# Activations of the gated and plain expert stages go to SBUF instead of back into their PSUM bank

## The reference, cut to what matters

```python
x = x + _L0_attn_ref(_layernorm(x), ...);  x = x + _L0_ffn_ref(_layernorm(x), ...)
x = x + _L1_attn_ref(_layernorm(x), ...);  x = x + _L1_ffn_ref(_layernorm(x), ...)
x = x + _L2_attn_ref(_layernorm(x), ...);  x = x + _L2_ffn_ref(_layernorm(x), ...)
x = x + _L3_attn_ref(_layernorm(x), ...);  x = x + _L3_ffn_ref(_layernorm(x), ...)
```

```python
# layer 0: 64 experts of width 64, two share a chunk of 128 rows; one shared expert without a routing weight
expert_act = silu(x @ gate[e]) * (x @ up[e])
routed = sum_e((expert_act * router_mask[..., e]) @ down[e])      # + shared expert
# layer 1: 8 experts of width 128
out = sum_e(cw[:, e] * (square(relu(x @ w1[e])) @ w2[e]))
# layer 2: 4 experts of width 512 (16 chunks of 128)
out = sum_i(w_i * (relu(x @ W1[e_i] + b1[e_i]) @ W2[e_i] + b2[e_i]))
# layer 3: 8 experts of width 128
out = sum_e(weights[..., e] * ((silu(x @ Wg[e]) * (x @ Wu[e])) @ Wd[e]))
```

## Time and profile before

| | us |
|---|---|
| median of 3 runs | 2436.68 |
| the profiled execution's own time | 2446.33 |
| its span | 2444.6 |
| PE busy | 1734.2 |
| DVE busy | 1528.8 |
| ACT busy | 1033.7 |
| POOL busy | 827.6 |

### The profile page before, as it was taken

The page is one execution under the profiler, slowest core; times in us unless marked ns, Lnnn a source line. Parts: engine busy times, 40 slices in busy tenths (PEclk is TensorE's granted clock), DMA queues, the critical chain, the costliest instruction groups (busy, mean ns, idle before and its releaser), DMA issues. The chain is left out here.

```text
span 2444.6 us, 31503 instructions
## 1 busy us (share of the span) xinstructions
PE 1734.2 (71%) x9106; PEld 1310.7 (54%) x9106; DVE 1528.8 (63%) x3384; ACT 1033.7 (42%) x1728; POOL 827.6 (34%) x717
## 2 busy tenths in 40 slices
PE   2903455666999999999577757767779994443599
PEld 2903355434777777777355535545546663222387
DVE  6787422355766666666546757767765566988566
ACT  0308400224544555554345635543447772222454
POOL 2020000002555555555300005530038783222255
PEclk9955565777999999999757758878879997665699
DMA  1001488106755555545100006430011111000355
GB/s 37 13 9 62 145 279 288 63 11 140 152 111 110 113 113 110 115 108 109 42 18 1 1 6 122 104 80 1 1 27 43 34 34 26 0 1 1 69 121 120
DMA packets 144435, 179.55 MB, mean 73 GB/s; under 512 B 37527, under 2 KB 89051, under 8 KB 144379
## 3 DMA queue, kind: packets, MB, share of 16 engines
q1 hardware_dynamic: 142568, 178.47, 30.5%
q10 hardware_dynamic: 1810, 0.42, 0.1%
HBM read 174.53 MB, written 4.33 MB: 73 GB/s over the span
## 5 line engine op out<-in xcount | busy, mean ns | idle before, releaser
L794 POOL TENSOR_TENSOR ffn_alo<-ffn_a,ffn_ahi 128x512 fp32r<-128x512 f32 x520 | 669.6, 1290 | 509.3 <-ACT ffn_ahi L755 505.6
L821 DVE TENSOR_TENSOR ffn_a<-ffn_G,ffn_mask 128x512 f32<-128x512 f32 x384 | 264.8, 690 | 241.6 <-ACT ffn_G L763 218.6
L763 ACT ACTIVATE ffn_G<-ffn_G 128x512 f32<-128x512 f32 x384 | 223.5, 582 | 359.0 <-PE ffn_G L104 356.9
L755 ACT ACTIVATE ffn_ahi<-ffn_a 128x512 fp32r<-128x512 f32 x520 | 324.7, 624 | 32.9 <-DVE ffn_a L825 29.0
L102 PE MATMUL ypsum<-ffn_ahi,ffn_hi 128*128 128x512 f32 x520 | 228.1, 439 | 48.7 <-POOL ffn_alo L794 34.9
L102 PE MATMUL ffn_G<-xn_hi,ffn_hi 128*128 (+1 forms) x520 | 220.8, 425 | 31.3 <-DVE ffn_lo L801 27.5
L825 DVE TENSOR_TENSOR ffn_a<-ffn_U,ffn_a 128x512 f32<-128x512 f32 x320 | 221.4, 692 | 29.7 <-DVE ffn_a L821 0.5
L194 POOL TENSOR_TENSOR ln_var<-ln_moments,eps 128x4 f32<-128x4 f32 x56 | 11.1, 199 | 671.2 <-DVE ln_moments L174 671.2
L103 PE MATMUL ffn_G<-xn_lo,ffn_hi 128*128 (+1 forms) x520 | 214.4, 412 | 0.0
L104 PE MATMUL ffn_G<-xn_hi,ffn_lo 128*128 (+1 forms) x520 | 213.8, 411 | 0.0
L103 PE MATMUL ypsum<-ffn_alo,ffn_hi 128*128 128x512 f32 x520 | 210.6, 405 | 0.0
(11 more groups left out here) (509 smaller groups left out, 3788.0 us busy)
## 6 DMA issues: line engine op xcount, KB each, us to landing
ffn_mask<-mask_rows_top SPq DMA_DIRECT2D x128, 512.0 KB, 6.8
rec_T<-scratch_kernels SPq DMA_DIRECT2D x32, 1536.0 KB, 7.7
ffn_mask<-mask_rows_top SPq DMA_DIRECT2D x16, 1024.0 KB, 8.2
ffn_mask<-mask_rows_zone SPq DMA_DIRECT2D x16, 1024.0 KB, 8.3
ffn_mask<-mask_rows_steps SPq DMA_DIRECT2D x16, 512.0 KB, 4.7
x<-in_L_attn_x SPq DMA_DIRECT2D x8, 256.0 KB, 4.8
ffn_raw<-in_L_ffn_expert_gate_k SPq DMA_DIRECT2D x16, 128.0 KB, 3.3
ffn_raw<-in_L_ffn_expert_up_k SPq DMA_DIRECT2D x16, 128.0 KB, 3.4
```

Of the source, the lines that this page charges most:

```text
L755: act.activation(ahi[i][:, :], a[i][:, :], ACT.Copy).then_inc(k.ahi_done, 1)
L763: act.activation(gate if masked(c) else a[c % RING_A][:, :], gate, how, **kw).then_inc(k.r_done, 1)
L794: eng.tensor_tensor(alo[i][:, :], a[i][:, :], ahi[i][:, :].bitcast(F32), ALU.subtract).then_inc(k.alo_done, 1)
L821: dve.tensor_tensor(out, gate[:, :], mask(c), ALU.mult).then_inc(k.t_done, 1)
```

## The change

In ffn0, ffn2 and ffn3 the activation is written to the chunk's buffer `a` in SBUF, and the first multiplication of DVE reads `a` and the mask, both in SBUF, and writes `a` in place. ffn1 stays as it was (`in_bank`). Two waits move with it: the wait for `alo_done` of chunk c - RING_A goes from DVE to ACT, ahead of the activation, and PE may write into a G bank as soon as the activation of the chunk RING_G before is done (`r_done`), no longer after DVE's multiplication. The wait of the up product for `a_done` stays.

```diff
+        in_bank = s.kind == "relu2"
         scaled = k.t_done if s.kind != "relu" else k.a_done
...
                     if exists(g, c, RING_G):
-                        if gated:
-                            pe.wait_ge(k.t_done, mid0 + g * C + c - RING_G + 1)
+                        if in_bank:
+                            pe.wait_ge(k.a_done, at(g, c) - RING_G + 1)
                         else:
-                            pe.wait_ge(k.a_done, at(g, c) - RING_G + 1)
+                            pe.wait_ge(k.r_done, at(g, c) - RING_G + 1)
...
                 def activate(g, c):
                     gate = banks(c)[0][:, :]
-                    if not masked(c) and exists(g, c, RING_A):
+                    if not in_bank and exists(g, c, RING_A):
                         act.wait_ge(k.alo_done, at(g, c) - RING_A + 1)
                     act.wait_ge(k.g_done, at(g, c) + 1)
                     kw = {"bias": bias1[:, c:c + 1]} if bias1 is not None else {}
-                    act.activation(gate if masked(c) else a[c % RING_A][:, :], gate, how, **kw).then_inc(k.r_done, 1)
+                    act.activation(gate if in_bank else a[c % RING_A][:, :], gate, how, **kw).then_inc(k.r_done, 1)
...
-                    if exists(g, c, RING_A):
+                    if in_bank and exists(g, c, RING_A):
                         dve.wait_ge(k.alo_done, at(g, c) - RING_A + 1)
+                    active = gate[:, :] if in_bank else out
                     if s.kind == "relu":
-                        dve.tensor_tensor(out, gate[:, :], mask(c), ALU.mult).then_inc(k.a_done, 1)
+                        dve.tensor_tensor(out, active, mask(c), ALU.mult).then_inc(k.a_done, 1)
                         return
-                    dve.tensor_tensor(out, gate[:, :], mask(c), ALU.mult).then_inc(k.t_done, 1)
+                    dve.tensor_tensor(out, active, mask(c), ALU.mult).then_inc(k.t_done, 1)
```

## The result

The changed kernel takes 2462.5 us in the median of 20 runs, the kernel before 2434.7 in as many beside it: a ratio of 1.010, 95% interval 1.0081 to 1.0119, so 20 to 29 us slower, 24 in the middle; the two medians themselves lie 27.8 us apart. The forecast was slower by 31 us, 2468 us, with a range of 2440 to 2502.

The account below looks back on a forecast made before the run. PE was taken to bound ffn0, ffn2 and ffn3, with DVE's two SBUF inputs contending with POOL deciding the change. ffn2 +25, ffn0 +7, ffn3 -0.7 sum to +31 us on 2436.7: 2468 us, range 2440 to 2502.

Parts of the forecast that it names:

- ffn3's -0.7: Start of ffn3: PE can do the third chunk's gate product before the late mask, -0.7 us, bounds -3.8 and 0.
- A pair costs 1.66 us: One DVE multiplication with two SBUF inputs plus one POOL subtraction, both engines always having work: 0.54 + 1.12 = 1.66 us.
- The sum of ffn2, +25: ffn2: +2.0 per group x 8 = +16, plus +1.3 at L181 for 7 groups = +9; bounds +6 and +75.
- One sign of being right: ffn2: PE was to wait for `alo` by some 20 us more than before.
- ffn0, +7: ffn0: multiplication falls into POOL's gap, leaving three terms of +2, +3 and +2 us; bounds 0 and +17.
- The part for the chunks behind the statistics, +3: ffn0, behind DVE's statistics, L181 and L216: later multiplication delays POOL 0.12 us x 3 places x 8 groups = +3.
- the +2 for it: ffn0: activation into SBUF takes 598 ns against 582; 8 ns a chunk x 264 = +2 us.
- the +2 at the inverse root: ffn0, where POOL is late already and PE waits 2.28 us: 0.25 us added a group, +2.
- Absorbed: Rival, 0.19: ffn2's multiplications slip into POOL's pauses as in ffn0; +2 to +8 us, 2441.
- Full blocking: Rival, 0.10: the second instruction waits, then takes its whole duration; 1.98 us a pair, ffn2 group 34.1 us, 2528 us.
- Clock: Rival, 0.06: ffn2's new waits drop PE's clock to 1.2 GHz once a group, +13 us on top, 2481.
- Faster: Rival, 0.05: gate bank given back 0.7 us earlier lets PE run ahead in ffn0, with ffn3 -15 us, 2422.

## Why the prediction was right, point by point

**The early bank release gives nothing.** Right. With ffn2 as before, the change in ffn0 and ffn3 has a ratio of 0.9987 with 1 inside the interval. ffn3's -0.7 did not show in the stages (0.0): PE's one wait of 3.8 us moved to the up product at its full length.

```profile
PE ffn_U L102 <- DVE ffn_a L827: 3.8, 1, 3.8
```

**A pair costs 1.66 us where both engines always have work.** Right: 15.12 / 9 = 1.68. The rows of an attention part with other operations on the same sizes carried over to this one, in both directions: a blocked multiplication ends 0.54 behind POOL's end, a blocked subtraction 1.14 behind DVE's.

**The sum of ffn2, +25.** Right in mechanism and, at +24.1, in size, but the nearness of the total is partly luck: a loop group was set 0.6 us too high, 4 us over seven groups, and the first group 3 us too low. A group was to take 29.0 us and 1.3 more in those with a normalisation, 30.3; it takes 29.7. The pause at the turn was set at 1.2 and is 1.46, the late chunk behind L181 at 1.3 and is a pause of 1.29. What was too high is POOL's busy time, 27.8 against 26.75: not all 16 multiplications are blocked, the one beside L196 (1872.16) takes 0.69, and three subtractions in a row in front of the late one need 1.26 each, as before. L194 on the other side is held too, 0.65 us where it took 0.20 before; that was not in the sum. The first group takes 5.0 us more from the attention's last copy to its own (60.5 against 55.5) where the sum gave it +2.0; which of its splits and multiplications make that up was not taken apart.

One sign of being right did not come as stated. PE was to wait for `alo` by some 20 us more in ffn2. By the profile it waits 8.3 us for `alo` (7.2 before) and 9.8 for `ahi` (0.8 before), the latter once a group behind the late multiplication, up to 1.3 us; the rest is spread in waits of some 0.2 us in front of the down products.

**ffn0, +7.** This term was mis-sized, and two of its three parts failed. The part for the chunks behind the statistics, +3, is the one that came. Four subtractions a group take 1.38 us and not 1.29 (754.10, where the prediction had worked out 0.12 more for just such a chunk), and the chunk behind each is 0.08 to 0.10 us longer. That is about 0.35 a group, all of what the undisturbed groups grew by (74.5 to 74.8 us). The activation's 16 ns were right in duration (598 against 582), but the other chunks of a group together did not grow, so the +2 for it does not show. Nor does the +2 at the inverse root: PE's wait there is 2.3 us as before, and L196 does not hold the multiplication inside it (0.69 to 0.70 us in all seven loop groups).

In the profile ffn0 even came out at -1.8. What hides the growth is the clock: the stall at the root was followed by a fall of the granted clock, some 1.5 us each, in four of the seven groups before and in two after. Whether the change has a part in that isn't settled. The other kernel with the change in ffn0, that with ffn2 as before, has two falls as well; the two with ffn0's activation in PSUM (the change in ffn2 alone, the wait alone moved) have four and three; each is one profile. The sign "within 1.5 us of 77" was set from a wrong base, too: 538 / 7 counts a window that runs on behind the last group, and the groups before took 75.2 on average.

**The rivals.** Absorbed: no, the mean multiplication of ffn2 is 1258 ns. Full blocking at 1.98 a pair: no, 1.68. Clock: a middle group of ffn2 kept 1.00 with PE's waits of up to 1.3 us in it. Faster: no. The forecast of 31 us lies 7 above the 24 of the ratio and of the stage table, and that is mostly the ffn0 term; it lies 3 above the 27.8 between the medians, so the runs don't fix the miss to the microsecond.

## What to carry to other kernels

Before moving an operand of VectorE from PSUM to SBUF, look at what GpSimd does at that time. If both inputs are in SBUF, the instruction and GpSimd's SBUF reads exclude each other, and there are two questions. Does the pair still fit the period of a chunk together with GpSimd's other work and pauses? In ffn2 it did not: 1.68 us a pair in a chunk of 1.69 left nothing for the inverse root and the turn of the group. And where does the instruction fall against GpSimd's? In ffn0, with 2.2 us a chunk, nearly all multiplications fell into POOL's gap; pushed onto the subtraction by a fill, they cost 5 to 6 us a group, though the pair is shorter than the chunk. In ffn3, with the same fill, a group kept its 17.2 us, so even this loss depends on what slack the stage has. Look for such a pair elsewhere in the same trace: it gives the price in both directions. And look at what stands behind a waiting instruction in GpSimd's list: one entry of a table was worth 18 us, with the same instructions.

## What the runs showed of the hardware that had not been expected

- Who goes first is not decided by the start of the rows. Behind a fill on DVE, a multiplication that started 0.62 us inside POOL's subtraction ran unhindered in 0.62 us and the subtraction took 2.38; behind L181, one that started 0.05 us inside it waited to its end. The cause is open.
- POOL's power function L196 on 128x4 did not hold a VectorE instruction with two SBUF inputs in its 1.01 us (0.69 to 0.70 us each time, in the 14 loop groups of ffn0 and ffn2), while the short addition L194 before it was itself held in ffn2's seven, 0.65 us in place of 0.20.
- A blocked instruction shows its waiting as duration and not as idle time before it: DVE's busy time in ffn2's window rose from 140.2 to 200.1 us with fewer instructions in it (247 for 271). One form with two mean durations, 691 and 1258 ns, was the sign.
- The activation with a bias is slower into SBUF than into PSUM by 26 ns (688 against 662), that without by 16 (598 against 582).
